# A five-sweep graph network: row degrees summed over partitions on VectorE, a row's own operands transposed in pairs, sweep 4's last product as a transpose, constants loaded later

## The reference

```python
h = relu(layernorm(x))                       # layer 0
for k in range(2):
    h = tanh(concat([adj @ h, h], 1) @ W0[k])
x = x + h
h = relu(layernorm(x))                       # layer 1
x = x + adj @ (h @ W1) + bias
h = relu(layernorm(x))                       # layer 2
x = x + adj @ (h * (u >= 0.1) / 0.9)
h = relu(layernorm(x))                       # layer 3
neigh = adj @ h / (adj.sum(axis=1) + 1)
x = x + concat([h, neigh], 1) @ W3.T
```

## Time and profile before

| | |
|---|---|
| median of 3 runs (lowest, highest) | 2417.26 us (2416.97, 2418.13) |
| the profiled execution | 2418.83 us |
| its span, first to last instruction | 2415.8 us |
| PE busy | 2366.0 us (98%) |
| PE weight loads busy | 1183.3 us (49%) |
| DVE busy | 1009.7 us (42%) |
| ACT busy | 141.5 us (6%) |
| granted TensorE clock | 1.00 of full speed |
| DMA | 820.88 MB, mean 340 GB/s |
| windows of 50 us, 150 to 650 us: DMA busy share | 0.91 to 0.97 |
| the same windows: DVE busy | 24 to 32 us of 50 |
| windows of 50 us, 1250 to 1650 us: DVE busy | 33 to 42 us of 50 |

### The profile page before, as it was taken

The page is one execution under the profiler, slowest core; times in us unless marked ns, Lnnn a source line. Parts: engine busy times, 40 slices in busy tenths (PEclk is TensorE's granted clock), DMA queues, the critical chain, the costliest instruction groups (busy, mean ns, idle before and its releaser), DMA issues.

```text
span 2415.8 us, 24269 instructions
## 1 busy us (share of the span) xinstructions
PE 2366.0 (98%) x9920; PEld 1183.3 (49%) x9920; DVE 1009.7 (42%) x2073; ACT 141.5 (6%) x315; POOL 13.4 (1%) x23
## 2 busy tenths in 40 slices
PE   5999999999999999999999999999999999999998
PEld 3544545454455444444454444444444544444665
DVE  6855546555453211100078787876411110005211
ACT  1000000000001311100010000000000000000000
POOL 0000000000000000000000000000000000000000
PEclk9999999999999999999999999999999999999999
DMA  9999999999997788888868888886899999999998
GB/s 386 421 416 352 370 355 364 353 363 347 361 365 287 276 285 292 298 294 301 339 258 341 295 301 301 311 317 261 310 376 370 360 374 355 361 374 370 357 422 351
DMA packets 118638, 820.88 MB, mean 340 GB/s; under 512 B 14593, under 2 KB 18817, under 8 KB 19329
## 3 DMA queue, kind: packets, MB, share of 16 engines
q1 hardware_dynamic: 113904, 814.79, 88.2%
q10 hardware_dynamic: 3856, 2.46, 0.3%
q0 software_dynamic: 768, 2.10, 0.3%
HBM read 817.20 MB, written 2.10 MB: 339 GB/s over the span
## 4 chain that ended last, share of the span: by engine, by line
PE 93%; DMA 5%; DVE 1%; issue 0%; ACTq 0%; ACT 0%; POOL 0%; DVEq 0%; SPq 0%; POOLq 0%
PE double_acc L591 56%; PE spare L591 12%; PE single_acc L567 12%; PE spare L567 8%; DMA ring<-in_adj 5%; PE natural L637 2%; PE spare L653 1%; PE spare L615 1%; PE natural L641 1%; DMA ones_sb<-in_ones 1%; DVE centred L750 0%; DVE stats L738 0%; DVE deg_part L780 0%; DVE deg_part L779 0%; DVE moments L741 0%
## 5 line engine op out<-in xcount | busy, mean ns | idle before, releaser
L591 PE MATMUL double_acc<-ring,operand 128*128 128x512 f32 x3144 | 1371.7, 594 | 2.9 <-DVE operand L890 1.3
L591 PEld LDWEIGHTS double_acc<-ring,operand 128*128 128x128 f32 x3144 | 589.1, 190 | 720.3 <-issue 713.1
L567 PE MATMUL single_acc<-ring,operand 128*64 128x256 f32 x3008 | 355.4, 385 | 39.1 <-DMA ones_sb<-in_ones 21.6
L819 DVE TENSOR_TENSOR sums<-double_acc,sums 64x256 f32<-64x256 f32 x120 | 50.7, 422 | 752.5 <-PE double_acc L591 751.6
L591 PE MATMUL spare<-ring,operand 128*128 128x512 f32 x672 | 298.9, 597 | 0.0
L567 PEld LDWEIGHTS single_acc<-ring,operand 128*64 128x64 f32 x3008 | 205.5, 137 | 185.5 <-issue 36.8
L780 DVE TENSOR_TENSOR deg_part<-deg_part,ring 128x1024 f32<-128x1024 f32 x214 | 262.1, 1225 | 7.3
L779 DVE TENSOR_TENSOR deg_part<-deg_part,ring 128x1024 f32<-128x1024 f32 x214 | 261.9, 1224 | 7.3 <-DMA ring<-in_adj 0.9
L792 DVE TENSOR_TENSOR partial<-spare,partial 64x256 f32<-64x256 f32 (+1 forms) x190 | 80.4, 423 | 290.6 <-PE spare L591 144.6
L591 PEld LDWEIGHTS spare<-ring,operand 128*128 128x128 f32 x672 | 124.3, 190 | 152.2 <-issue 152.2
L567 PE MATMUL spare<-ring,operand 128*64 128x256 f32 x1456 | 163.5, 381 | 0.7 <-DVE partial L792 0.7
(11 more groups left out here) (54 smaller groups left out, 583.3 us busy)
## 6 DMA issues: line engine op xcount, KB each, us to landing
ring<-in_adj SPq DMA_DIRECT2D x756, 1024.0 KB, 6.7
held<-in_adj SPq DMA_DIRECT2D x17, 1024.0 KB, 8.8
resid<-in_x SPq DMA_DIRECT2D x16, 128.0 KB, 10.2
kept<-in_adj SPq DMA_DIRECT2D x2, 1024.0 KB, 9.7
for_layer<-in_u POOLq DMA_DIRECT2D x16, 128.0 KB, 2.4
out_rows<-for_layer ACTq DMA_DIRECT2D x16, 128.0 KB, 6.9
w_both_sb<-in_w_both ACTq DMA_DIRECT2D x2, 80.0 KB, 7.9
w_own_sb<-in_w_own ACTq DMA_DIRECT2D x2, 32.0 KB, 8.9
```

What stands on the lines that cost most here:

```text
L567: last = nc.tensor.matmul(acc[half_of(h), 0:HALF], operand[:, b.j * TPB + t, half_of(b.row.half)], stream[:, t, nodes_of(h)], start=b.firs ...
L591: last = nc.tensor.matmul(acc[:, :], operand[:, b.j * TPB + t, :], stream[:, t, :], start=b.first and t == 0, stop=b.last and t == TPB - 1)
L819: last = nc.vector.tensor_tensor(to, got[own, nodes_of(h)], to, ALU.add)
```

## The change

1. **Degrees.** At the end of a row VectorE transposes the folded 128 x 512 sums in 32 x 32 squares and reduces each square's columns: 128 x 16 numbers into `deg_quarter`. What is left is a sum over four groups of 32 partitions. It is done once for all rows, after the last, by two PE products with a 0/1 matrix `fold_sb`, made on VectorE from the identity at the start of sweep 3. The 32 `degree` groups, the column of ones and its load are gone; one `degrees` stands at the place of the last.
2. **Own operands.** ScalarE copies the row's own half of `operand` into `own_by_pair` (128 x 2 x 128), two pieces beside each other. `turn` transposes 2 instead of 4, and `own_t` is one 128 x 256 copy instead of two of 64 x 256. The copy for the next row stands on ScalarE right behind the `own_t` copy. POOL's clearing of `operand` is gone.
3. **Place of `turn` in sweep 1.** It stands directly ahead of `post`, after the second single block; row 0's comes after the ninth.
4. **Sweep 4's `post`** is two transposes instead of two products with an identity.
5. **Constants.** ScalarE issues the eight loads after two square roots instead of nine ahead of them, and PE waits for them only at its first `turn`.

```diff
 def make_plan():
 ...
+            if n == (min(1, len(row.single) - 1) if row.r else NB // 2):
+                plan.append(("turn", row))
+                if row.r:
+                    plan.append(("post", ROWS[row.r - 1]))
 ...
             def turn(row):
-                wait_operand(wait_new, row.sweep, row.i)
+                wait_new(consts_loaded, 16 * CONSTS)
+                wait_new(own_paired, rows_with_own(row.r))
                 acc = next_spare()
-                wait_new(cleared, 1)
-                for t in range(TPB):
-                    last = nc.tensor.transpose(acc[:, t * P:(t + 1) * P], operand[:, row.i * TPB + t, :], ident[:, :])
+                for k in range(2):
+                    last = nc.tensor.transpose(acc[:, k * P:(k + 1) * P], own_by_pair[:, k, :], ident[:, :])
 ...                                                                  # in post
+                    if row.sweep == 4:
+                        last = nc.tensor.transpose(to[:, 0, k], sums[:, row.r % 2, cut], ident[:, :].rearrange("p (h f) -> p h f", h=2))
+                        continue
 ...
-            def degree(row):
-                wait_new(deg_folded, DEGREE_ROWS.index(row) + 1)
+            def degrees():
+                wait_new(fold_made, 1)
+                wait_new(deg_squared, len(DEGREE_ROWS))
                 acc = next_spare()
-                for t in range(TPB):
-                    part = deg_part[:, DEGREE_ROWS.index(row) % 2, t * P:(t + 1) * P]
-                    last = nc.tensor.matmul(acc[:, t:t + 1], part, ones_sb[:, :], start=True, stop=True)
+                for part in range(2):
+                    last = nc.tensor.matmul(acc[:, 0:NB * SQUARES], fold_sb[:, :],
+                                            deg_quarter[:, part].rearrange("p i b -> p (i b)"), start=part == 0, stop=part == 1)
 ...
-            wait_new(consts_loaded, 16 * CONSTS)
 ...                                                                  # ScalarE
+            def pair_own(row):
+                wait_operand(act.wait_ge, row.sweep, row.i)
+                own = operand[:, tiles(row.i), half_of(row.half)].rearrange("p (h k) f -> p k h f", k=2)
+                nc.scalar.copy(own_by_pair[:, :, :].rearrange("p k (h f) -> p k h f", h=2), own).then_inc(own_paired, 1)
 ...
-                    for h in range(2):
-                        last = nc.scalar.copy(own_t[half_of(h), slot, :], spare[use % 2][own, nodes_of(h)])
-                    last.then_inc(own_ready, 1)
+                    nc.scalar.copy(own_t[:, slot, :], spare[use % 2][:, 0:HALF]).then_inc(own_ready, 1)
+                    if row.i != (0 if row.sweep == SWEEPS else NB - 1 if row.sweep == 1 else 0):
+                        pair_own(ROWS[row.r + 1])
 ...                                                                  # VectorE, behind the fold L784
+                    nc.vector.transpose(acc[:, BLOCK:], acc[:, 0:BLOCK]).then_inc(deg_turned, 1)
+                    dve.wait_ge(deg_turned, folds[0])
+                    nc.vector.reduce_sum(deg_quarter[:, degree_half(b.row), b.row.i, :],
+                                         acc[:, BLOCK:].rearrange("p (b c) -> p b c", c=SQUARE),
+                                         axis=mybir.AxisListType.X).then_inc(deg_squared, 1)
 ...
+            def make_folding():
+                dve.wait_ge(consts_loaded, 16 * CONSTS)
+                link(nc.vector.reduce_sum(lane[:, :], ident[:, :].rearrange("p (q r) -> p r q", q=QUARTERS),
+                                          axis=mybir.AxisListType.X))
+                nc.vector.tensor_copy(fold_sb[:, :].rearrange("p (q r) -> p q r", q=QUARTERS),
+                                      lane[:, :].unsqueeze(1).to_broadcast([P, QUARTERS, SQUARE])).then_inc(fold_made, 1)
```

More of the change, by code:

```diff
@@ L41 @@
 TPB = BLOCK // P
+SQUARE = 32
+QUARTERS = P // SQUARE
+SQUARES = BLOCK // SQUARE
 HALF = BLOCK // 2
@@ L67 @@
 OWN_WEIGHTS = {1: 0, 5: 1, 2: 2}
-CONSTS = 9
+CONSTS = 8
 class Row:
@@ L206, in make_plan @@
             count[0] += 1
[L207 to L210, removed]
             if row.r and n == min(3, len(row.single) - 1):
@@ L280, with degree_half @@
 DEGREE_ROWS = [row for what, row in PLAN if what == "degree"]
+def degree_half(row):
+    return 0 if row.sweep == 1 else 1
 class Load:
@@ L353, in kinds_with_banks @@
         kind = "added" if what == "added_both" else what
-        if kind in ("added", "turn", "degree"):
+        if kind in ("added", "turn") or what == "degree" and of is DEGREE_ROWS[-1]:
             found.append((kind, counts.get(kind, 0)))
@@ L412, in gnn_kernel @@
         ident = sb("ident", [P, P])
-        ones_sb = sb("ones_sb", [P, 1])
+        fold_sb = sb("fold_sb", [P, P])
+        lane = sb("lane", [P, SQUARE])
         sums = sb("sums", [P, 2, HALF])
         own_t = sb("own_t", [P, 2, HALF])
-        deg_part = sb("deg_part", [P, 2, 2 * BLOCK])
-        deg_plus = sb("deg_plus", [P, NT])
+        own_by_pair = sb("own_by_pair", [P, 2, 2 * F])
+        deg_part = sb("deg_part", [P, 2 * BLOCK])
+        deg_quarter = sb("deg_quarter", [P, 2, NB, SQUARES])
+        deg_plus = sb("deg_plus", [P, NB, TPB])
         rdeg = sb("rdeg", [P, NT])
@@ L664, in _, with deviation @@
                     multiply[of.kind](of).then_inc(blocks_used, 1)
-                elif what in ("turn", "post", "degree"):
-                    {"turn": turn, "post": post, "degree": degree}[what](of)
+                elif what in ("turn", "post"):
+                    {"turn": turn, "post": post}[what](of)
+                elif what == "degree" and of is DEGREE_ROWS[-1]:
+                    degrees()
         @block.scalar
         def _(act):
+            deviations = [0]
+            def deviation(n, slot):
+                deviations[0] += 1
+                act.wait_ge(var_ready, deviations[0])
+                nc.scalar.activation(sd[:, slot, 0:n], moments[:, slot, 0:n, 1], ACT.Sqrt, bias=eps[:, 0:1]).then_inc(sd_ready, 1)
+            def pair_own(row):
+                wait_operand(act.wait_ge, row.sweep, row.i)
+                own = operand[:, tiles(row.i), half_of(row.half)].rearrange("p (h k) f -> p k h f", k=2)
+                nc.scalar.copy(own_by_pair[:, :, :].rearrange("p k (h f) -> p k h f", h=2), own).then_inc(own_paired, 1)
+            act.wait_ge(eps_set, 1)
+            for g in range(2):
+                deviation(GROUP, g % 2)
             act.wait_ge(weights_cleared, 2)
@@ L714, in _ @@
                         nc.scalar.activation(to, got, ACT.Tanh).then_inc(tanh_ready, 1)
+                        if row.r == NB - 1:
+                            pair_own(ROWS[NB])
                     if row.sweep in (2, 3, 4):
@@ L846, in take_both, with take_degrees @@
                 last.then_inc(added_taken, 1)
-            def take_degrees(row):
-                count = DEGREE_ROWS.index(row)
-                dve.wait_ge(deg_summed, count + 1)
-                got = spare[SPARE_USES.index(("degree", count)) % 2][:, 0:TPB]
-                to = deg_plus[:, tiles(row.i)]
-                if row.sweep == 1:
-                    nc.vector.tensor_scalar_add(to, got, 1.0).then_inc(deg_taken, 1)
-                else:
-                    dve.wait_ge(deg_taken, count)
-                    nc.vector.tensor_tensor(to, got, to, ALU.add).then_inc(deg_taken, 1)
-                if row is DEGREE_ROWS[-1]:
-                    dve.wait_ge(deg_taken, count + 1)
-                    link(nc.vector.reciprocal(rdeg[:, :], deg_plus[:, :]))
+            def take_degrees():
+                dve.wait_ge(deg_summed, 1)
+                got = spare[SPARE_USES.index(("degree", 0)) % 2][:, 0:NB * SQUARES]\
+                    .rearrange("p (i t q) -> p i t q", i=NB, q=QUARTERS)
+                for q in range(QUARTERS):
+                    part = slice(q * SQUARE, (q + 1) * SQUARE)
+                    last = nc.vector.tensor_scalar_add(deg_plus[part], got[part, :, :, q], 1.0)
+                last.then_inc(deg_taken, 1)
+                dve.wait_ge(deg_taken, 1)
+                link(nc.vector.reciprocal(rdeg[:, :], deg_plus[:, :, :].rearrange("p i t -> p (i t)")))
             def finish(row):
@@ L927, in _ @@
                     finish(of)
-                elif what == "degree":
-                    take_degrees(of)
+                elif what == "degree" and of is DEGREE_ROWS[-1]:
+                    take_degrees()
 def kernel(x, adj, L0_gnn_W, L1_gnn_weight, L1_gnn_bias, L2_gnn_u, L3_gnn_W):
```

28 lines of the change are left out of this document (14 added, 14 removed).

## The result

| | before | changed | difference |
|---|---|---|---|
| median of 4 runs each (lowest, highest) | 2417.7 us (2416.97, 2418.35) | **2377.49 us** (2376.13, 2377.71) | -40.2 us |
| ratio, 95% interval | | 0.9833 (0.9821, 0.9845) | 1.7% less time |
| the profiled execution | 2418.83 us | 2377.46 us | |
| its span | 2415.8 us | 2375.3 us | -40.5 us |

The account below looks back on a forecast made before the run. PE was taken to bound the kernel from 93 to about 2285 us, loads both ends; 25.3 + 9.5 + 3.5 = 38.3 us off the median of 2417.26 gives 2379.0 us, likeliest 2376 to 2382, whole range 2375 to 2386.

Parts of the forecast that it names:

- What bounds the kernel: PE's work counts in full from 93 to about 2285 us; in the load-bound stretches at both ends it counts nothing.
- Part 1, degrees: Removing the 32 degree groups from PE's path, with `degrees` in place of the last, gains 25.3 us.
- the term of sweep 3: Sweep 3: 14 degree groups at 0.81 us, 11.3 us, less 0.4 for a wait in row 3, gain 10.9 us.
- The two exceptions: Sweep 3's row 3 loses 0.4 us waiting for its operand; sweep 4's first group gains nothing, as `post` awaits a copy.
- The last group's replacement: `degrees`, four instructions of 256 columns, costs the same 1 us (bounds 0.5 and 2); the VectorE instructions behind are hidden.
- Part 2, `turn`: Two transposes fewer and the new place gain 9.5 us in sweeps 1, 2 and 5; the new ScalarE copy is hidden.
- Part 3, sweep 4: Sweep 4's `post` with two transposes instead of products: 16 rows at 0.22 us, gain 3.5 us.
- Part 4, the constants: At the start PE begins at about 10 us instead of 21.64, worth 0 (bounds -1 and +1 us), since loads are full.
- Part 5, VectorE: VectorE's 32 new transposes and reductions cost PE nothing; in sweep 3's short rows its slack is 0.8 us at worst.
- T: VectorE's time for one transpose and reduction of 128 x 512 together, taken as 1.4 us, between 1.15 and 2.8 us.
- The prediction's working for larger T: Sweep 3's short rows: PE would lose from T = 1.8 us, about 3 us at 2.8; that rival's chance 0.08.
- its formula: Sweep 3, rows 3 to 13: loss about (T - 0.5)^2 / 1.8, eating 38 us from T = 9 us; chance 0.03.

Follow-up runs that it names:

- e10: Changed kernel with 64 more transposes on PE in rows 24 and 25, in the middle of sweep 2: 2384.57 us, ratio 0.9864.
- e9: Changed kernel with 64 more transposes on PE in rows 0 and 1, before 93 us: 2377.34 us, ratio 0.9834.
- e2: Kernel before with the degree sums alone changed (transposed and reduced on VectorE, one pair of products at the end): 2390.43 us, ratio 0.9889.
- e3: Kernel before with `own_by_pair` and two transposes a row instead of four, `turn` at its old place: 2410.03 us, ratio 0.9970.
- e4: Kernel before with `turn` moved to `post`'s place in sweep 1, still four transposes: 2415.29 us, ratio 0.9991.
- e1: Changed kernel with PE waiting for the constants before its first block, constants still issued late: 2381.35 us, ratio 0.9852.
- e6: Changed kernel with each row's transpose and reduction done twice on VectorE: 2382.64 us, ratio 0.9856.
- e7: Changed kernel with each row's transpose and reduction done four times on VectorE: 2407.78 us, ratio 0.9964.

## Why the prediction was right

- **What bounds the kernel: right.** PE between 93 us and the tail. e10 shows that work there moves the end by its full price (7.1 us for 64 transposes), e9 that the same work moves nothing before.
- **Part 1, degrees: right, and the term of sweep 3 too small.** e2 gives 26.8 us for 25.3. The prediction took the distance inside the old order, 0.81 us, for what a group costs. In the traces rows 4 to 14 of sweep 3 give 0.89 us each and the last 0.95: without the group the doubles on both sides are one run, and the joint saves 0.08 us. The prediction had counted that joint between single blocks (0.16 us) and left it out between doubles. Eleven times 0.08 us and the last row's 0.14 are 1.0 of the 1.5 us that were missing; the rest is spread over both ends and is no more than the runs' spread. The two exceptions came as worked out: row 3 of sweep 3 gave 0.41 us for the forecast 0.4, and the start of sweep 4 nothing. There the 1.0 us of the group turned into a wait for the same copy, as PE and VectorE show beside the earlier trace rows:

```profile
1669.38 0.29 DVE L848 COPY sums<-partial 128x256 f32<-128x256 f32 x1
...
1669.73 0.44 PE L651 MATMUL natural<-ident,sums 128*128 128x128 f32 x2 [0.95 <-DVE sums L848]
```

- **The last group's replacement: right.** Four products of 256 columns cost 2232.76 - 2231.70 = 1.06 us, for the 1 us taken (bounds 0.5 and 2):

```profile
2231.70 1.13 PE L669 MATMUL spare<-deg_quarter,fold_sb 128*128 128x256 f32 x4
...
2232.76 1.95 PE L580 MATMUL single_acc<-ring,operand 128*64 128x256 f32 x16
```

- **Part 2, `turn`: right.** e3 and e4 give 7.2 + 2.0 = 9.2 us for 9.5. The new ScalarE copy is nowhere on PE's path: no wait of PE names it in the changed kernel or in e3.
- **Part 3, sweep 4: right.** 3.7 us for 3.5, and 0.22 us to the next double.
- **Part 4, the constants: right at 0, for a reason that was nearly used up.** The prediction argued that the loads were full. e1 shows that this holds only while PE begins before the ring is full: with its start 5.7 us later than in the kernel before, 3.9 us are lost.
- **Part 5, VectorE: right.** T is 1.40 us for the 1.4 taken from the fold's row. The estimate of 1.9 us made from the Trainium skill, VectorE: DVE Perf Modes, "The three transpose paths", was too high: one 128 x 512 float32 transpose takes 0.711 us, not four times 311 ns. The page gives that figure for 128 x 128 alone, and the factor of four was the prediction's. And its rule in "Rules for kernel authors" that `tensor_reduce` is the slowest VectorE operation did not bite here: 0.686 us for 512 columns, beside 0.692 for the addition of as many. That the work fits is shown at T = 1.4; e6 shows that at twice that it costs 5 us. The prediction's working for larger T was 2 us small there and 15 at T = 5.8, where it had neither sweep 1's tight row nor the lower clock. It also slipped in a sum: at T = 9.5 its formula gives 45 us and so 2424 us, not 2421. Nothing in the forecast rests on that.

## What to carry to other kernels

Before pricing a saving, divide the bottleneck engine's time into stretches by what it waits for: work removed inside a load-bound stretch is worth nothing (e9), outside it is worth its full distance and also the joint that its removal makes between the neighbours. Work moved to an idle engine costs nothing up to an edge that the tightest rows set, not that engine's mean share; look for them in every sweep. Beyond it the bottleneck engine can lose more than it waits, since long waits here came with a lower clock (e7). Where one end of a kernel is load-bound and the part before it is not, moving blocks across the border pays the difference of the two rates; here that was worth another 13.7 us.

## What the runs showed of the hardware

- A float32 STREAM_TRANSPOSE of 128 x 512 takes VectorE 0.711 us, about the time of an addition of 512 columns (0.692 us).
- A group of small products between larger ones costs PE more than its own distance: between doubles 0.89 us went with the group where its own distance was 0.81 us, and in e2 rows whose group stood between two single blocks gained 1.13 us where the others gained 0.89. Of 34 transposes in a row each costs 3.71 / 34 = 0.11 us.
- The granted clock of PE fell from the full 2.4 GHz to 1.2 GHz for a few microseconds beside each of five waits of 2.8 to 4.3 us in e7 (the windows of 10 us show mixtures of both levels, 0.66 for example), and beside none of e6's waits for sums, 1.4 us at most. In the changed kernel it was 0.70 in the window 35 to 40 us, where PE worked in bursts (3.08 us of it) and had just waited 2.32 us; the double of row 1 came no later than the loads let it.
- PE's first block takes twice the usual time in both kernels: 3.68 us in the kernel before, from 21.64 us on, instead of 1.95, at a granted clock of 1.00 by the windows. The 5.46 us of the changed kernel's first row are such a block and one of the usual length, which began only at 13.35 us when its operand was there. The first block's weight loads stand 0.43 us apart, as they do in the block at 36.92 us where the granted clock is at its lower level; why the windows read 1.00 is open.
